# A top-k masked feed-forward layer and a quantized-LoRA layer on one core: PSUM banks by parity, a third cast amid the signs, w2 loaded piece by piece

## The reference, cut to what matters

```
# x: (2, 1024, 1024), all float32; I = 2752
def first(x, w_gate, w_up, w_down):
    s = silu(x @ w_gate.T)                     # (tokens, 2752)
    # the k = I // 2 = 1376 entries of a row that are smallest in magnitude become 0
    _, idx = top_k(-abs(s), I // 2);  s[rows, idx] = 0
    return (s * (x @ w_up.T)) @ w_down.T
def second(x, w1q, a1, b1, w3q, a3, b3, w2q, a2, b2):
    lin = lambda x, wq, A, B: x @ tile(wq, (1, 4)).T + 0.5 * (x @ A.T @ B.T)
    return lin(silu(lin(x, w1q, a1, b1)) * lin(x, w3q, a3, b3), w2q, a2, b2)
x = layernorm(x + first(x, ...))
x = layernorm(x + second(x, ...))
```

## Time and profile before

| | us |
|---|---|
| median of 3 runs (lowest, highest) | 1971.96 (1970.97, 1975.37) |
| the profiled execution: its time / its span | 1973.22 / 1971.4 |
| TensorE busy, granted clock over the span | 1932.7, 0.997 |
| DVE, ACT, POOL busy | 1243.3, 733.5, 923.4 |

### The profile page before, as it was taken

One profiled execution on the slowest core, in us unless ns is written; L12 is line 12 of the kernel. 1 busy time (PEld: TensorE's weight loads), 2 busy tenths in 40 slices (PEclk: granted clock), 3 DMA queues, 4 the chain that ended last, 5 costly groups with the idle time before them and its releaser, 6 DMA issues. The chain is left out here.

```text
span 1971.4 us, 24654 instructions
## 1 busy us (share of the span) xinstructions
PE 1932.7 (98%) x9320; PEld 1615.6 (82%) x9320; DVE 1243.3 (63%) x1782; ACT 733.5 (37%) x1184; POOL 923.4 (47%) x746
## 2 busy tenths in 40 slices
PE   9999999999999999999999999999999999999998
PEld 7897978978889897788888978889788777887776
DVE  2147975689864337897532489865016998469963
ACT  4356443473333335523243463233232342113312
POOL 5456884446556544455464445544573432013310
PEclk9999999999999999999999999999999999999999
DMA  4333432224334323434243324333443132212212
GB/s 144 94 99 91 121 104 85 88 91 139 102 121 136 94 88 98 137 98 131 81 142 94 99 86 139 97 127 117 160 140 103 43 117 97 73 56 75 97 43 86
DMA packets 102114, 203.67 MB, mean 103 GB/s; under 512 B 11492, under 2 KB 27876, under 8 KB 100688
## 3 DMA queue, kind: packets, MB, share of 16 engines
q1 hardware_dynamic: 97384, 185.28, 30.4%
q10 hardware_dynamic: 4608, 16.78, 2.1%
HBM read 185.24 MB, written 16.78 MB: 102 GB/s over the span
## 5 line engine op out<-in xcount | busy, mean ns | idle before, releaser
L515 POOL TENSOR_TENSOR wl<-w_in_place,wh 128x512 fp32r<-128x512 f32 (+2 forms) x552 | 716.8, 1303 | 659.4 <-ACT wh L646 658.7
L646 ACT CAST wh<-w_in_place 128x512 fp32r<-128x512 f32 (+2 forms) x560 | 327.6, 591 | 777.0 <-DMA w_in_place<-in_wu 295.6
L1337 PE MATMUL banks<-wh,xTh 128*128 128x512 f32 (+2 forms) x1536 | 566.2, 369 | 7.3 <-POOL wl L515 6.4
L1339 PE MATMUL banks<-wh,xTl 128*128 128x512 f32 (+2 forms) x1536 | 563.4, 367 | 0.0
L1338 PE MATMUL banks<-wl,xTh 128*128 128x512 f32 (+2 forms) x1536 | 563.3, 367 | 0.0
L1337 PEld LDWEIGHTS banks<-wh,xTh 128*128 128x128 f32 x1536 | 288.4, 188 | 50.2 <-POOL wl L515 9.2
L1339 PEld LDWEIGHTS banks<-wh,xTl 128*128 128x128 f32 x1536 | 288.3, 188 | 40.2
L1338 PEld LDWEIGHTS banks<-wl,xTh 128*128 128x128 f32 x1536 | 288.4, 188 | 39.4
L1337 PE MATMUL banks<-wh,hTh 128*128 128x512 f32 x672 | 264.8, 394 | 14.5 <-POOL wl L515 14.4
L1338 PE MATMUL banks<-wl,hTh 128*128 128x512 f32 x672 | 262.4, 390 | 0.0
L1339 PE MATMUL banks<-wh,hTl 128*128 128x512 f32 x672 | 262.4, 390 | 0.0
(11 more groups left out here) (144 smaller groups left out, 2201.3 us busy)
## 6 DMA issues: line engine op xcount, KB each, us to landing
w_in_place<-in_wd SPq DMA_DIRECT2D x176, 256.0 KB, 2.6
w_in_place<-in_wg SPq DMA_DIRECT2D x128, 256.0 KB, 2.6
w_in_place<-in_wu SPq DMA_DIRECT2D x128, 256.0 KB, 2.6
w_in_place<-in_w SPq DMA_DIRECT2D x54, 256.0 KB, 2.8
x_in_place<-in_xT SPq DMA_DIRECT2D x32, 256.0 KB, 3.8
y<-in_xtok SPq DMA_DIRECT2D x4, 2048.0 KB, 8.5
x<-y ACTq DMA_DIRECT2D x16, 512.0 KB, 4.1
xa<-x SPq DMA_DIRECT2D x16, 512.0 KB, 4.1
```

What stands on the lines that cost most here:

```text
L515: nc.gpsimd.tensor_tensor(lo, landed, hi.bitcast(F32), ALU.subtract).then_inc(done, 1)
L646: nc.scalar.copy(hi, piece).then_inc(hi_done, 1)
L1337: nc.tensor.matmul(dst, ah, bh, start=start, stop=False)
L1339: return nc.tensor.matmul(dst, al, bh, start=False, stop=stop)
```

## The change

1. Chunk j of gate and up takes banks `2 * t + j % 2`: all even or all odd ones. The transposes and all readers follow. The waits follow as well: down's first piece needs the banks of the last chunk but one, its second piece (d = 1) those of the last; up's first chunk needs only the adds of n = 0, tile by tile, its second those of n = 1. In the last down, d = 0 waits for the transposes' low parts of set 4, d = 1 for those of set 5.
2. `search` casts after `(2, 0)`, `(2, 1)` and `(3, 0)` for every b, and behind the semaphore 1, 2, 2, 1, 1, 1 pieces in the six rounds for b of 1 to 3 (26 pieces in all, 24 before); b = 0 keeps its three and two.
3. In the last down SP issues weight piece d first, then one w2 piece at each odd d from 5 to 27, the small inputs at d = 8, `load_b` at 12, the two x1 tiles at 14 and 16, x at 24 (before: 25).
4. The clearing and the small memsets go from POOL to DVE, behind its last `turned`.

```diff
             for d in range(ND):
+                load_d(NB - 1, d)
                 if d == 5:
-                    load_w2()
-                if d == 6:
+                    sp.wait_ge(pe_used, LAST_D)
+                if 5 <= d < 5 + 2 * NW2 and d % 2:
+                    load_w2((d - 5) // 2)
+                if d == 8:
                     load_small()
-                if d == 7:
-                    load_xa(0, 0)
-                    load_xa(0, 1)
-                if d == 9:
+                if d == 12:
                     load_b()
-                if d == 25:
+                if d in (14, 16):
+                    load_xa(0, (d - 14) // 2)
+                if d == 24:
                     x_tiles(NB - 1)
-                load_d(NB - 1, d)
...
-                            if (t, h) in amid:
+                            if t == 2 or h == 0:
                                 piece()
...
-                    for _ in range(behind):
+                    for _ in range(behind[r]):
                         piece()
...
-                search(b, lambda: high_d(b - 1, next(ahead)), ((2, 0), (3, 0)), 2)
+                search(b, lambda: high_d(b - 1, next(ahead)), (1, 2, 2, 1, 1, 1))
...
-                        bank = 4 * j + t
-                        pe.wait_ge(d_evac, 8 * (b - 1) + 4 * (bank % 2) + bank // 2 + 1)
+                        pe.wait_ge(d_evac, 8 * (b - 1) + 4 * j + t + 1)
...
-                        if d < 2 and t >= 2 or d == t == 0:
-                            bank_waits(2 * t + n)
+                        if d < 2:
+                            bank_waits(t, n)
...
-                down(b - 1, lambda bank: silu_taken(b, max(bank + 1, 4)))
+                down(b - 1, lambda t, n: silu_taken(b, 4 * n + t + 1))
...
-            down(NB - 1, lambda bank: turned(NB - 1, NJ - 2 if bank < 4 else NJ - 1))
+            down(NB - 1, lambda t, n: turned(NB - 1, NJ - 2 + n))
...
-                            ins = nc.tensor.transpose(banks[4 * p + m][0:rows, t * P:(t + 1) * P], h, ident[:, :])
+                            ins = nc.tensor.transpose(banks[2 * m + p][0:rows, t * P:(t + 1) * P], h, ident[:, :])
```

More of the change, by code:

```diff
@@ L319, in program @@
         xa_in = [sem(f"xa_in{i}") for i in range(2)]
-        small_in, b_zero, b_in, b_ready, split_ready, sel_ready = (
-            sem("small_in"), sem("b_zero"), sem("b_in"), sem("b_ready"), sem("split_ready"), sem("sel_ready"))
+        small_in, b_zero, b_in, b_ready, sel_ready = (
+            sem("small_in"), sem("b_zero"), sem("b_in"), sem("b_ready"), sem("sel_ready"))
         l_fold = sem("l_fold")
@@ L404, in _, with load_w2 @@
                 load_up(b)
[L406 to L411, removed]
+            def load_w2(d):
+                rows = rows_of(d // 2)
+                sp.dma_start(w2_in_place[0:rows, d // 2, (d % 2) * 512:(d % 2 + 1) * 512],
+                             w2[d // 2, 0:rows, (d % 2) * 512:(d % 2 + 1) * 512]).then_inc(w2_raw[d], 16)
             def load_small():
@@ L574, in _ @@
                 low_d(NB - 1, d)
[L575 to L598, removed]
                 if d >= ND - NW2:
@@ L671, in evac @@
                     dst = s0[:, in_chunk(j, t)] if b == 0 else v[:, t, cols(j)]
-                    nc.scalar.activation(dst, banks[4 * (j % 2) + t][:, 0:width(j)], ACT.Silu).then_inc(g_freed, 1)
+                    nc.scalar.activation(dst, banks[2 * t + j % 2][:, 0:width(j)], ACT.Silu).then_inc(g_freed, 1)
             def gate(b):
@@ L684, in gate, with search @@
                             turned(b - 1, NJ - 1, 1)
-            def search(b, piece, amid, behind):
+            def search(b, piece, behind):
                 for r in range(ROUNDS):
@@ L709, in turned @@
                         act.wait_ge(x1_out, 16 * NT * b)
-                    nc.scalar.copy(hTh[:, c, :], banks[4 * p + m][:, :]).then_inc(t_hi, 1)
+                    nc.scalar.copy(hTh[:, c, :], banks[2 * m + p][:, :]).then_inc(t_hi, 1)
             def up(b):
@@ L751, in copy_u @@
                         act.wait_ge(pe_used, up_at(0) + KH * (j + 1))
-                    nc.scalar.copy(w0[:, in_chunk(j, t)], banks[4 * (j % 2) + t][:, 0:width(j)]).then_inc(u0_copied, 1)
+                    nc.scalar.copy(w0[:, in_chunk(j, t)], banks[2 * t + j % 2][:, 0:width(j)]).then_inc(u0_copied, 1)
             def up_0(i):
@@ L764, in _ @@
             ahead = iter(range(3, NG))
-            search(0, lambda: up_0(next(ahead)), ((2, 0), (2, 1), (3, 0)), 2)
+            search(0, lambda: up_0(next(ahead)), (2, 2, 2, 2, 2, 2))
             for i in ahead:
@@ L1139, in take_up @@
                             dve.wait_ge(pe_used, up_at(b) + KH * (j + 1))
-                        V.tensor_tensor(s, banks[4 * (j % 2) + t][:, 0:width(j)], s, ALU.mult).then_inc(u_freed, 1)
+                        V.tensor_tensor(s, banks[2 * t + j % 2][:, 0:width(j)], s, ALU.mult).then_inc(u_freed, 1)
                     if j < NJ - 1:
@@ L1156, in turned @@
                     dve.wait_ge(t_hi, NC * b + c + 1)
-                    V.tensor_tensor(hTl[0:rows, c, :], banks[4 * p + m][0:rows, :],
+                    V.tensor_tensor(hTl[0:rows, c, :], banks[2 * m + p][0:rows, :],
                                     hTh[0:rows, c, :].bitcast(F32), ALU.subtract).then_inc(t_lo, 1)
@@ L1190, in _, with fill @@
                 take_up(b)
+            def fill(part, value):
+                step(V.memset(part, value))
+                st.done()
+            dve.wait_ge(t_done, NC * NB)
+            V.memset(braw[:, :], 0.0).then_inc(b_zero, 1)
+            V.memset(b2raw[0:LR, :], 0.0).then_inc(b_zero, 1)
+            for part, new, old, n in ((split_b, (LORA, -1.0), (0.0, 1.0), 2 * R), (split_x, (1.0, -1.0), (0.0, 1.0), R)):
+                for i in range(2):
+                    fill(part[:, i:i + 1], old[i])
+                    for p0 in QUAD:
+                        fill(part[p0:p0 + n + R, i:i + 1], new[i])
+                        fill(part[p0:p0 + n, i:i + 1], old[i])
+            fill(sel[:, :, :], 0.0)
+            for r in range(R):
+                V.memset(sel[:, r, :].rearrange("p (g k) -> p g k", g=3)[:, :, r:r + 1], 1.0).then_inc(sel_ready, 1)
             dve.wait_ge(small_in, 16 * 2)
             dve.wait_ge(b_ready, 2)
-            dve.wait_ge(split_ready, 1)
             step(V.tensor_scalar(braw[0:LX, :], braw[0:LX, :], split_b[0:LX, 0:1], None, ALU.mult))
@@ L1353, in chunk @@
                         tt = slice(t * P, (t + 1) * P)
-                        ins = three(banks[4 * (j % 2) + t][:, 0:width(j)], xTh[:, i, tt], xTl[:, i, tt], wh[:, w],
+                        ins = three(banks[2 * t + j % 2][:, 0:width(j)], xTh[:, i, tt], xTl[:, i, tt], wh[:, w],
                                     wl[:, w], i == 0, i == KH - 1)
```

## The result

| | before | after |
|---|---|---|
| median of 4 runs, us | 1972.36 (1970.97 to 1975.37) | 1958.87 (1958.14 to 1959.49) |
| the profiled execution: time / span, us | 1973.22 / 1971.4 | 1959.35 / 1957.6 |

What follows compares the result with a forecast made beforehand. It took TensorE as the bound, busy 1932.7 of 1971.4 us. Downs beside searches -1.1, clock +3.9, last down -4.2 sum to -1.4 us: 1971.8 for the profiled execution, 1970.6 as median, range 1964 to 1976.

Steps and rivals of the forecast that it cites:

- the third cast: Search, b = 1 to 3: rounds grow 0.39 us, six by 2.34; casts behind the semaphore free; with restarts -1.1 us.
- The wait for the search at the start of up: Before up's first chunk: TensorE waits for the first add, 3.5 us for b = 1 and 2, 6.1 for b = 3.
- TensorE's own part of the three downs: Downs beside the searches: matmuls take 120.5 us; for b = 1 they end at 498.5, 4.5 us sooner than 503.0.
- 3.9 for three: Starts of up, b = 1 to 3: clock falls behind TensorE's new gaps, 1.3 us each, +3.9; ends 0 and 4.9.
- The banks' edit: Start of up: tile 1 needs the second add, not the fifth; without it the longer search costs 1.8 us more each time.
- The last down: Last down: all 5.2 us over its matmuls go, except a new wait of 1.0 at piece 13: -4.2 us.
- its rival's: Last down: `load_b` makes piece 13 late, a wait of 4.3 us and a clock fall; +4.5 in all, 1976.5, chance 0.12.
- remark on the two-row DMAs: Last down: all twelve `braw` DMAs share two engines, so piece 13's wait is nearer its upper end, 4.3 us.
- the rival of the free cast: Search, b = 1 to 3: third cast costs nothing, up starts 2.34 us sooner thrice; -11.0 us, 1961, chance 0.06.
- In full: All four downs: every TensorE gap goes, 26 us, giving 1946; chance 0.02.
- The clock did not hold: Starts of up: the rival that TensorE's clock does not fall there; -5.3 us, 1966.7, chance 0.22.

Runs made afterwards that it cites:

- e1: The kernel before with only the search part of the change (three casts amid the signs, 1, 2, 2, 1, 1, 1 behind): 1966.07 us, ratio 0.9977.
- e6: The changed kernel with the eighteen DMAs of `load_b` issued six at a time, at d = 12, 16 and 20: 1953.89 us, ratio 0.9915 to before.
- e10: The changed kernel run again unaltered, on the same chip as two other follow-up runs: 1957.96 us, ratio 0.9929 to before.
- e2: The kernel before with only the banks part of the change (banks by parity, with their waits): 1971.77 us, ratio 0.9998.
- e3: The kernel before with only SP's new load order in the last down and the memsets on DVE: 1970.82 us, ratio 0.9997.
- e5: The changed kernel, POOL waiting for DVE's next trial before subtracting pieces behind the signs (rounds 0 to 4, b = 1 to 3): 1949.57 us, ratio 0.9889 to before.
- e4: The kernel before with 0, 1, 2, 3, 1, 2 pieces behind the signs in the six rounds of b = 1 to 3: 1984.77 us.
- e9: The changed kernel with `load_b` issued six DMAs at a time and POOL waiting for DVE's next trial in the searches of b = 0 to 3: 1940.30 us, ratio 0.9843.

## Why the prediction was wrong

**The step that failed** is the one on the third cast, in its last clause: that the casts behind the semaphore "lie beside DVE's small steps [...] and cost nothing". The cast itself costs nothing there; the subtraction that POOL makes of it holds DVE for 1.0 us. I took a round of b = 0 (12.03 us) for the new form, because it has three casts amid the signs, and did not see that it has two behind while four of the six new rounds have one. The sum for such a round is 11.64 + 0.39 - 1.0 = 11.03, and 11.04 was measured. So the six rounds do not grow by 2.34 us. The five distances from trial to trial sum to 57.3 us, 58.3 before, instead of 60.2. Everything behind that step moved with it: the search of b = 1 ended at 120.5 and not 123.2 us.

For b = 2 and 3 it ended at 117.7 and 120.5 us, where the same sum gives 123.3 and 125.9. The rounds explain 3.0 of these 5.7 and 5.4 us. The rest is the exact pick, which I had taken to stay as long as it was: in these two blocks its steps were held for less than before. The forecast had no term for it. From the sixth trial to the first add the three blocks together take 171.9 us in the changed kernel, 172.4 in e1, 171.5 in e6 and 172.9 in e10, and 175.6, 178.1 and 174.9 in before, e2 and e3. So the sum goes with edit 2; which block has the shorter one does not, as e10 shows, and that it was b = 2 here, which then had no wait, is chance.

The rows that show the failed step stand in the profile of before, in the same view as the earlier trace rows: 1.17 and 1.15 us for steps of eight columns. I read the round's length and its one idle time and not the durations in between.

The Trainium skill has the rule: "SBUF — State Buffer", section "Who interferes with whom", says that a VectorE instruction with two inputs in SBUF and a GpSimd instruction that reads SBUF want the same pair of ports, an exclusive lock held for the whole instruction, and that the loser is blocked. The runs agree: the held steps of a round have two inputs in SBUF, they end with POOL's instruction (1.29 us), and take 1.15 to 1.17 us instead of 0.15 to 0.17.

**What held.** The wait for the search at the start of up and what frees it (the first add) were as forecast for b = 1 and 3, 2.0 us instead of 3.5 and 6.1, since the search was earlier. TensorE's own part of the three downs was forecast to end at 120.5 us and ended at 119.2, 119.0 and 119.1: in a round of 11.04 us the first piece of a round is late by less. The clock fell behind both waits that were there, to 0.76 over 7 us, which is 7 x 0.24 = 1.7 us each; I had charged 3.9 for three and 3.4 was paid for two. That this term came out nearly right is luck: in e10, the same kernel, nothing was paid behind waits of 1.88 and 2.00 us, and nothing in e6 behind 1.82 and 1.87. The banks' edit did what it says, and e1 puts about 4 us on it.

**The last down** was mis-sized. The mechanism was the one named, and its rival's: piece 13 behind `load_b`. I had 10.6 us from the first of its DMAs to the cast, by taking the backlog out of the 14.1; it was 1398.21 - 1385.69 = 12.5 (11.4 in e3, 12.8 in e10, 13.2 in e5). TensorE waited 3.2 us and the clock fell (0.76 over 7 us, 1.7 us), so this down saved 0.1 and not 4.2. The forecast's remark on the two-row DMAs leaned to the upper end of the wait, 4.3, and had the direction right; no row shows single DMA engines. e6 shows that both are the burst of `load_b`: the gap is away when it comes in three parts.

**The rivals.** The time lies at the rival of the free cast (1961), but not by its mechanism: the third cast does cost 0.4 us, and the rounds with two behind took 12.0 to 12.2. What it shares is its consequence, a search that does not end later. "In full" was excluded rightly. The clock did not hold in the profiled execution, and held at both waits of e10.

**Left open.** The second layer is 2.3 us shorter. In the kernel before the clock fell at 1899, behind a wait of 1.7 us for `t2s`; in the changed kernel it did not, with a wait of 1.4 us there. That wait is 1.7 us in all four kernels without edits 3 and 4 (before, e1, e2, e4) and 1.3 or 1.4 in all with them, so these edits seem to bear on it; how is not shown. Of the four with 1.7, e1 had no fall. Nor does any run tell what decides on a fall: the same wait of 2.40 us in up 0, at 190, was followed by one in e6 and not in the kernel before. Why the exact pick is held for less with edit 2, and in one block more than in another, is open as well.

## What to carry to other kernels

Before an engine's short steps are called free, read their durations and not only their gaps: a step seven times as long as its like is held by somebody, and the instruction on the other engine that ends at the same time says by whom. Work of POOL that nobody waits for at once can be put behind DVE's chain of short steps by one wait a round. Here that was worth about 8 us in the searches of b = 1 to 3, and with b = 0 (e9 against e6, 0.9843 against 0.9915) 14, as much as the whole change. When a burst of narrow DMAs is moved, what is queued behind it moves along: split the burst so that each part fits into the slack of the piece behind it.

## What the runs showed of the hardware

- A step of DVE over 2 to 8 columns takes 0.15 to 0.2 us alone and up to 1.3 us when it begins beside a POOL tensor_tensor of 128x512 (1.29 us). A step with two inputs of 1376 columns takes 1.65 us alone and 2.40 to 2.71 beside one. Not only steps with two inputs in SBUF are held: in b = 0 of the kernel before, with POOL busy back to back, three TENSOR_SCALAR steps with one input took 1.22, 1.22 and 1.21 us. The 48 counts over 2752 columns with an accumulator took 3.07 to 3.08 us, with or without POOL beside them. DVE in b = 0:

```profile
179.34 1.22 DVE L952 TENSOR_SCALAR sadd<-sadd 128x2 f32<-128x2 f32 x1
180.59 1.22 DVE L955 TENSOR_SCALAR tc<-sadd 128x2 f32<-128x2 f32 x1
181.84 1.21 DVE L970 TENSOR_SCALAR le<-tc 128x8 f32<-128x8 f32 x1
```

- Eighteen DMAs of two rows each (12 of 21.8 KB, 6 of 8 KB) were issued in 5.4 us, and the cast of the piece loaded behind them came 12.5 us after the first issue (11.4 to 13.2 in the other kernels with this order). Behind six of them it came after 5.7 us.
- An idle time of TensorE of about 2 us may or may not be followed by a fall of its clock. 1.98 and 1.99 us (changed kernel) were each followed by a granted clock of 0.76 over 7 us, between the levels of 1.2 and 2.4 GHz, which costs 1.7 us; 1.88 and 2.00 us (e10), 2.06 (e3) and 2.62 (e1, last down) were followed by 1.00. Those of 3.21 (changed kernel), 3.54 (e10) and 3.87 us (e5) were all followed by a fall.
